# ScalarE in place of GpSimd for the interpolation's tents, in a fused two-layer attention and expert kernel

## The reference, cut to what matters

```python
scores = jnp.einsum('bqh,bkh->bqk', Q_char, K_sub) * scale
char2sub = jnp.einsum('bqk,bkh->bqh', jax.nn.softmax(scores, axis=-1), V_sub)
...
scores2 = jnp.einsum('bqh,bkh->bqk', Q_sub, K_char) * scale
sub2char = jnp.einsum('bqk,bkh->bqh', jax.nn.softmax(scores2, axis=-1), V_char)
L_char = char_emb.shape[1]
if sub2char.shape[1] != L_char:
    sub2char = _interp_linear(sub2char, L_char)
gate_in = jnp.concatenate([char2sub, sub2char], axis=-1)
gate = jax.nn.sigmoid(jnp.einsum('blh,oh->blo', gate_in, Wg) + bg)
return gate * char2sub + (1 - gate) * sub2char
```

## Time and profile before

| | before |
|---|---|
| median of 3 runs | 969.83 us (968.83 to 970.75) |
| profiled execution, its own time | 969.94 us |
| its span in the profile | 968.1 us |
| PE busy | 929.1 us, 96% |
| DVE busy | 731.4 us, 76% |
| ACT busy | 584.9 us, 60% |
| POOL busy | 352.6 us, 36% |
| TensorE clock granted, mean | 0.994 of full speed |

### The profile page before, as it was taken

The page is one execution under the profiler, slowest core; times in us unless marked ns, Lnnn a source line. Parts: engine busy times, 40 slices in busy tenths (PEclk is TensorE's granted clock), DMA queues, the critical chain, the costliest instruction groups (busy, mean ns, idle before and its releaser), DMA issues. The chain is left out here.

```text
span 968.1 us, 19310 instructions
## 1 busy us (share of the span) xinstructions
PE 929.1 (96%) x6934; PEld 876.1 (90%) x6934; DVE 731.4 (76%) x1711; ACT 584.9 (60%) x1248; POOL 352.6 (36%) x506
## 2 busy tenths in 40 slices
PE   9999999899999999999989999999999999999996
PEld 8899998678889999998778799999999999999995
DVE  6677777669577888885557666777657878998997
ACT  6346666433367777775244576666657766667653
POOL 5514545616324444432563200000000846545552
PEclk9999999999999999999999999999999999999999
DMA  8200000021278888881421200000010000000101
GB/s 248 88 1 1 1 2 1 1 87 66 71 254 253 273 265 260 261 259 40 134 59 37 88 1 1 1 1 2 1 44 19 7 1 13 23 23 23 34 13 34
DMA packets 50948, 72.38 MB, mean 75 GB/s; under 512 B 5488, under 2 KB 33776, under 8 KB 50864
## 3 DMA queue, kind: packets, MB, share of 16 engines
q1 hardware_dynamic: 45152, 55.81, 18.3%
q0 software_dynamic: 5024, 14.42, 4.5%
q10 hardware_dynamic: 688, 1.05, 0.3%
HBM read 59.34 MB, written 11.93 MB: 74 GB/s over the span
## 5 line engine op out<-in xcount | busy, mean ns | idle before, releaser
L2142 PE MATMUL wide<-V_hi,pt 128*128 128x258 f32 x400 | 116.3, 291 | 0.1
L2144 PE MATMUL wide<-V_hi,pt 128*128 128x258 f32 x400 | 113.4, 283 | 0.0
L2143 PE MATMUL wide<-V_lo,pt 128*128 128x256 f32 x400 | 113.0, 283 | 0.0
L2698 POOL TENSOR_SCALAR V_hi<-rows 128x256 fp32r<-128x256 f32 (+1 forms) x9 | 10.8, 1196 | 203.5 <-PE bank L2144 202.7
L2143 PEld LDWEIGHTS wide<-V_lo,pt 128*128 128x128 f32 x400 | 76.4, 191 | 0.2
L2142 PEld LDWEIGHTS wide<-V_hi,pt 128*128 128x128 f32 x400 | 75.9, 190 | 0.6 <-issue 0.2
L2144 PEld LDWEIGHTS wide<-V_hi,pt 128*128 128x128 f32 x400 | 76.2, 190 | 0.0
L43 PE MATMUL bank<-rx_hi,expert_w_hi 128*128 128x256 f32 x256 | 73.5, 287 | 1.5 <-PEq L1100 1.4
L45 PE MATMUL bank<-rx_hi,expert_w_lo 128*128 128x256 f32 x256 | 71.5, 279 | 0.0
L44 PE MATMUL bank<-rx_lo,expert_w_hi 128*128 128x256 f32 x256 | 71.5, 279 | 0.0
L503 POOL DMA_INDIRECT rxr<-token_rows,lists x39 | 56.8, 1456 | 29.1 <-issue 15.4
(11 more groups left out here) (539 smaller groups left out, 3598.7 us busy)
## 6 DMA issues: line engine op xcount, KB each, us to landing
sraw<-w1T SPq DMA_DIRECT2D x14, 512.0 KB, 4.8
sraw<-w3T SPq DMA_DIRECT2D x14, 512.0 KB, 5.2
sraw<-w2T SPq DMA_DIRECT2D x14, 512.0 KB, 5.0
raw_even<-w1T SPq DMA_DIRECT2D x11, 512.0 KB, 4.7
raw_even<-w3T SPq DMA_DIRECT2D x11, 512.0 KB, 5.1
raw_even<-w2T SPq DMA_DIRECT2D x11, 512.0 KB, 5.5
routed_results<-rys POOLq DMA_DIRECT2D x15, 256.0 KB, 4.5
X<-x SPq DMA_DIRECT2D x4, 512.0 KB, 6.5
```

What stands on the lines that cost most here:

```text
L2142: pe.matmul(dst[:, 0:D + 2], hi[:, x], v_hi(k), start=opens(n) and j == 0, stop=False)
L2143: pe.matmul(dst[:, 0:D], hi[:, x], v_lo(k), start=False, stop=False)
L2144: m = pe.matmul(dst[:, 0:D + 2], lo[:, x], v_hi(k), start=False, stop=closes(n) and k == keys_of(n)[-1])
L2698: pool.tensor_scalar(tent(i)[:, 0:n * P], d, 1.0, 0.0, ALU.add, ALU.max).then_inc(tent_done, 1)
```

## The change

Tents 1 to 14 are made by ACT instead of POOL. The position less the row number is taken apart: POOL copies the position (a column number times a constant, the same for all tiles) once into `where_kept`, and makes once 25 columns `off`, one for each tile and touched row tile, of (tile's shift - row number). ACT then makes |where_kept + off| with a bias per partition (`ACT.Abs`), once per touched tile, waits for that, and makes relu(1 - x) in place (`ACT.Relu`). Tiles 0 and 15 stay on POOL as they were, with a semaphore of their own, `edge_tent`. ACT's calls stand at the end of the steps in `TENTS_AT`: 59, 60, 61, and 63 + 7k // 2 for k = 0 to 10. From block 63 on, that is b = 0 and b = 3 of each group. Each stands 5 to 13 blocks ahead of the `interpolate` that needs it; the guard `between >= i - 5` is the same.

```diff
+                off = sb(ctx, "off", [P, 2 * NT])
+                where_kept = sb(ctx, "where_kept", [P, P])
...
+                TENTS_AT = [NSB + 3, NSB + 4, NSB + 5] + [first[SG + 1] + 7 * k // 2 for k in range(11)]
...
                     def interpolate(i):
-                        pe.wait_ge(tent_done, i + 1)
+                        if i == 0 or i == LAST:
+                            pe.wait_ge(edge_tent, 1 if i == 0 else 2)
+                        else:
+                            pe.wait_ge(tent_done, i)
...
+                    def tents_of(i):
+                        if i == 1:
+                            act.wait_ge(where_known, 1)
+                            act.wait_ge(edge_tent, 1)
+                        if i >= 6:
+                            act.wait_ge(between, i - 5)
+                        w = len(touching[i]) * P
+                        for k in range(len(touching[i])):
+                            act.activation(tent(i)[:, k * P:(k + 1) * P], where_kept[:, :], ACT.Abs,
+                                           bias=off[:, 2 * i + k:2 * i + k + 1]).then_inc(tent_far, 1)
+                        act.wait_ge(tent_far, sum(len(touching[j]) for j in range(1, i + 1)))
+                        act.activation(tent(i)[:, 0:w], tent(i)[:, 0:w].bitcast(F32), ACT.Relu, bias=1.0,
+                                       scale=-1.0).then_inc(tent_done, 1)
...
+                        if n in TENTS_AT:
+                            tents_of(1 + TENTS_AT.index(n))
...
-                        for k, rr in enumerate(touching[i]):
-                            x, row = apart[:, k * P:(k + 1) * P], row_f[:, rr:rr + 1]
-                            if middle:
-                                link(pool.tensor_scalar(x, where, at, row, ALU.add, ALU.subtract))
...
-                        link(pool.tensor_scalar(m, d, 0.0, -2.0, ALU.max, ALU.mult))
-                        link(pool.tensor_tensor(d, d, m, ALU.add))
...
+                    for i in range(1, LAST):
+                        for k, rr in enumerate(touching[i]):
+                            ins = pool.tensor_scalar(off[:, 2 * i + k:2 * i + k + 1], row_f[:, rr:rr + 1], -1.0, i * C * P / S,
+                                                     ALU.mult, ALU.add)
+                    link(ins)
+                    ins = pool.tensor_copy(where_kept[:, :], where).then_inc(where_known, 1)
+                    pool.wait_ge(where_known, 1)
                     tents_of(0)
-                    for i in range(1, 4):
-                        tents_of(i)
                     for i in range(11):
                         mix(i)
                         if i:
                             inverse(i - 1)
-                        if i < 10:
-                            tents_of(i + 4)
-                    tents_of(14)
                     mix(11)
```

More of the change, by code:

```diff
@@ L1945, in cross_phase @@
                          "weighted_done summed reciprocals finished")
-                (row_known, tent_step, tent_done, rows_high, rows_split) = sems(
-                    ctx, "row_known tent_step tent_done rows_high rows_split")
+                (row_known, tent_step, where_known, tent_far, edge_tent, tent_done, rows_high, rows_split) = sems(
+                    ctx, "row_known tent_step where_known tent_far edge_tent tent_done rows_high rows_split")
                 (between, copied, mixed, turned, in_high, in_low, gated, biased, squashed, scaled, moved, stat, gathered, inv, normal,
@@ L2681, in tents_of @@
                         d, m = apart[:, 0:n * P], apart_m[:, 0:n * P]
-                        at, middle = i * C * P / S, 0 < i < LAST
-                        if not middle:
+                        at = i * C * P / S
+                        if i == 0 or i == LAST:
                             link(pool.tensor_scalar(apart_m[:, 0:P], where, at, 0.0, ALU.add, ALU.max))
-                        for k, rr in enumerate(touching[i]):
-                            x, row = apart[:, k * P:(k + 1) * P], row_f[:, rr:rr + 1]
-                            if middle:
-                                link(pool.tensor_scalar(x, where, at, row, ALU.add, ALU.subtract))
-                            else:
-                                link(pool.tensor_scalar(x, apart_m[:, 0:P], float(C - 1), row, ALU.min, ALU.subtract))
-                        link(pool.tensor_scalar(m, d, 0.0, -2.0, ALU.max, ALU.mult))
-                        link(pool.tensor_tensor(d, d, m, ALU.add))
[L2693 to L2699, removed]
+                            for k, rr in enumerate(touching[i]):
+                                x, row = apart[:, k * P:(k + 1) * P], row_f[:, rr:rr + 1]
+                                link(pool.tensor_scalar(x, apart_m[:, 0:P], float(C - 1), row, ALU.min, ALU.subtract))
+                            link(pool.tensor_scalar(m, d, 0.0, -2.0, ALU.max, ALU.mult))
+                            link(pool.tensor_tensor(d, d, m, ALU.add))
+                            if i == 0:
+                                pool.wait_ge(unit_done, END)
+                                pool.wait_ge(weighted_done, NSB)
+                            else:
+                                pool.wait_ge(between, i - 5)
+                            pool.tensor_scalar(tent(i)[:, 0:n * P], d, 1.0, 0.0, ALU.add, ALU.max).then_inc(edge_tent, 1)
                     def mix(i):
```

## The result

The changed kernel takes 973.90 us (median of 6 runs, 972.43 to 974.91), the kernel before 969.59 (6 runs, 968.49 to 970.75). The ratio is 1.0046 (95% interval 1.0035 to 1.0057): **slower by 0.46%, 4.3 us**. The prediction was 971.4, within 968.8 to 974.3; the result lies in the range, near its upper end.

What follows compares the result with a forecast made beforehand. PE, busy 96% of the span, was taken to set the pace. Losses of 0.71 + 0.30 + 0.07 + 0.06 + 0.37 + 0.11 gave +1.6 us on the median of 969.83: 971.4 us, range 968.8 to 974.3.

Steps and rivals of the forecast that it cites:

- The prediction's own sign of being wrong: Wrong if L2821 stayed at 0.6 beside `mix`, PE had no gap near 778, or the end chain changed over 0.3 us.
- What is taken away: POOL's 14 tents, some 60 us, go; credited 0.17 to 0.22 us per DVE fold and 0.49 per L2944.
- rival B: Slower by more: dearer ACT tents, or `mix` colliding with the fold, up to 0.3 us per group; 972.5 to 975, chance 0.30.
- Item 1: Tent 3, before a full stretch of ACT (770 to 776), delays the first gate's weights: PE loses 0.71 us.
- Item 2: Tent 5, at 790.9, delays `evacuate` and DVE's work up to L2873, which PE awaits: PE loses 0.30 us.
- Price of a tent: A two-tile tent on ACT costs 0.70 + 0.03 + 0.30 = 1.03 us, bounds 0.7 and 1.5.
- Item 3: Tents 6, 8, 10, 12 at b = 0 delay DVE up to the fold by 1.00: PE loses 0, 0.07, 0.06, 0.37 us.
- Item 4: Tent 14, at b = 0 of the last group, where the room is 0: 0.11 us is left, carried into the end chain.
- Item 5: Odd tents from 7 on, at b = 3 before `keep_first` and 2.9 us of waiting for POOL, cost nothing.
- POOL's 26 early instructions: 25 column instructions and a copy on POOL, about 545 us, ahead of a 202.7 us wait, cost nothing.
- It is worth something where POOL slowed DVE: POOL's freed time gains only at slowed DVE rows: L2821 at 0.60 to 0.65 against 0.424, L2944 at 0.97 against 0.48.
- Rivals C and D: C: faster, DVE gains more from POOL's silence, 967.5 to 969.3, chance 0.12; D: ACT's delays absorbed, 969 to 970.3, 0.08.

Runs made afterwards that it cites:

- e5: The change with `mix` left out, one short POOL instruction signalling in its place: 971.49 us, ratio 1.0015.
- e1: The change, but `mix` of odd tiles 1 to 11 waits on POOL until DVE has folded the next group's maximum: 973.46 us, ratio 1.0033.
- e4: The change without ACT's tents: no engine makes tents 1 to 14, PE multiplies with tent 0's matrix instead: 970.35 us, ratio 1.0001.
- e6: e2 with tents 2 to 5 moved too: 2 and 3 to the ends of steps 64 and 65, 4 and 5 before `spread_max`: 970.12 us, ratio 1.0006.
- e2: The change with even tents 6 to 12 at b = 3 beside the odd ones, tent 14 in the closing order: 971.17 us, ratio 1.0009.
- e8: e6, with `mix(11)` alone waiting on POOL for the last group's fold: 969.37 us, ratio 1.0003.
- e7: The change with a second `Relu`, values unchanged, over tents 6, 8, 10, 12 and 14: 976.24 us, ratio 1.0069.
- e3: The kernel before, POOL's tents kept, with ACT's 39 instructions added in their places into an unread tile: 975.27 us, ratio 1.0053.

## Why the prediction was right and wrong

The direction was right, the forecast of 971.4 too small by 2.5 us (+1.6 against +4.3), and "within 0.2%" was given 0.55 where 0.46% came. That the result lies in the range is in part luck: the range reached up to 974.3 for tents of 1.5 us, and a tent takes 1.04. The prediction's own sign of being wrong did appear: L2821 (now L2841) did not come back to 0.43 but takes 0.83 to 0.85 with `mix` beside it. The cause rests on kernels that take the two suspects singly and together. Lost between 809.1 and 942.2:

```text
                             ACT not late   ACT late by a tent at b = 0
`mix` left out               not run        0.48 (e5)
`mix` held behind the fold   not run        1.91 (e1)
`mix` at once                0.05 (e4)      3.10 (change)
```

`mix` moved up costs 0.05 alone, ACT's delay 0.48 with POOL silent; together they cost 3.10. In a steady group the reason is in the rows: 1.00 of delay less the 0.18 by which a fold beside a silent POOL is shorter, and 0.25 of slow fold, each fit the room of 0.75 or nearly; 1.00 + 0.22 + 0.24 does not. That is why the sum of separate costs failed. "POOL off the fold" is not enough for the upper row: e1 has that too and loses 1.91, as `mix` then meets L2966.

- **"What is taken away": the step that failed.** "I credit 0.17 to 0.22 us per fold" assumed that, with the tents gone, POOL is silent there. The same change to POOL's queue lets `mix` start 3.6 us after the group's small exponential (834.16 against 830.57), where before it was 6.5, and so under L2837 and the fold. A credit of 0.17 became a charge of 0.22 + 0.24, up to 0.63 us too little in each of the groups from the second on (0.51 to 0.64 by the table). The prediction had seen this in rival B ("`mix`, now free to start when `copy` ends, collides with the fold"), with a price of up to 0.3, and left it out of the sum, although the working of B placed `mix(9)` over the fold by rows of before. What rows place there belongs in the sum.
- **Item 1 (tent 3, 0.71)**: right; gap 0.64, PE's load 0.75 later, gone in e6. **Item 2 (tent 5, 0.30)**: right; 0.35, gone in e6.
- **Price of a tent (1.03)**: right, 1.04. Rival B's dearer tents (1.15 and more) didn't come. Its other half did, and B's range of 972.5 to 975 holds the result, but B had put most of its loss on the tents' price and at most 0.3 per group on the collision.
- **Item 3 (0, 0.07, 0.06, 0.37)**: measured 0.15, 0.67, 0.70, 0.88 in the change; 0, 0.06, 0.05, 0.29 in e5, where POOL is silent as assumed. The delay, the rooms and the signal's 0.05 were right.
- **Item 4 (0.11)**: 0.70 in the change, 0.08 in e5. Same error: L2841 at 918.4 takes 0.83 and PE waits 1.69 for it. In the change PE also waits 0.36 at the `x_turn` ahead of it (917.35), since the tent delays `normalise` (L2508) too (the wait is absent in e2, e4, e6 and e8, and 0.45 longer in e7); the prediction didn't name it.
- **Item 5 (odd tents, 0)** and POOL's 26 early instructions (0): right; e2 has eight tents at b = 3 and loses 0.04 there.
- **"It is worth something where POOL slowed DVE"**: of the rows credited, only L2964 got shorter, and no turn of PE waits for it. With all tents gone (e4) the time is that of before, `mix` having moved up.
- **Rivals C and D**: out. e2 and e6 show D's mechanism, with the tents at places where ACT waits. The rule of the Trainium skill (GPSIMD Engine Reference, Specifications) that VectorE instructions with two SBUF inputs contend with GpSimd was put to rival C, as a gain. The trace agrees with the rule, but here the contention is a cost and not a gain: beside `mix`, L2905, one input in PSUM, keeps its 0.42, while L2837 right behind it, both in SBUF, goes from 0.41 to 0.63.

In e1 against e5 a second piece remains: with `mix` right behind the fold the last four groups lose 0.36 to 0.61 each, without it 0.05 to 0.29, some 0.3 to 0.5 more. In three of them 0.25 of it is PE's gap behind the slow L2966; the rest was not separated. The kernel that would fill the table, tents gone and `mix` left out or held, was not run either; the kernel before is near it, with its folds half slowed (0.60 to 0.65).

## What to carry to other kernels

Work taken from an engine's queue does not leave silence: what stood behind it moves up, so place the next instruction of that queue under the other engines' rows before crediting anything. Delays that use the same room have to be added up first and set against it once: where the room was 0.75 us, ACT's delay of 1.0 cost 0.06 alone (e5) and a slow fold nothing (e4), and together they cost 0.7. And one delay can make the other larger, as 0.22 of the 0.46 us on DVE came only because ACT was late. When work is moved to a queue, its place decides and not the queue's free share: put it just ahead of a wait longer than itself; the same 39 instructions cost 4.2 us in one set of places and 0.1 in another.

## What the runs showed of the hardware

- How much POOL slows a DVE operation with two SBUF inputs depends on POOL's own operation: a fold of 128 x 256 takes 0.42 alone, 0.60 to 0.65 beside a TENSOR_SCALAR that starts with it, and 0.83 to 0.87 beside a TENSOR_TENSOR (change, e3); a 128 x 512 one 0.68 alone and 1.22 beside the second step of `mix` (e4).
- It goes both ways: the first step of `mix` takes 0.74 when it meets DVE's L2905 and L2837, 0.92 when the fold lies under it (e4), and 1.07 when the 512-wide low part and L2966 do (e1).
- ACT's `Abs` with a bias per partition takes 0.39 us for 128 x 128, two of them 0.68 to 0.70, as long as L2428; `Relu` of 128 x 256 0.42.
